# Reordering the attention's first rounds: cross values, the quantised layer and the input roundings of batches 1 to 3

## What is computed

```python
x = x + _L2_xattn_ref(_layernorm(x), ctx, ctx, ...)            # layer 5, E in the kernel
x = x + _L2_ffn_ref(_layernorm(x), weight, bias)               # layer 6, F
x = x + _L3_xattn_ref(_layernorm(x), ctx, ...)                 # layer 7, G

# layer 6: rows scaled by their largest value, rounded to whole numbers, times ternary weights
scale = jnp.maximum(jnp.max(jnp.abs(x), axis=-1, keepdims=True), eps) / 127.0
q_x = jnp.clip(jnp.round(x / scale), -128.0, 127.0) * scale
out = jnp.einsum('bsi,oi->bso', q_x, q_w) + bias

# layer 7: four inputs, each divided by its scale and rounded to fp8, 8 head groups
q = _ln(_fp8_linear_pertensor(ln_out, wq, wq_scale, q_in_scale).reshape(b, s, g, hpg, d), ...)
k = _ln(_fp8_linear_pertensor(ln_out, wk, ...)); v = _fp8_linear_pertensor(ln_out, wv, ...)
core = _gqa(q, k, v)
qx = _ln(_fp8_linear_pertensor(ln_out, wqx, ...))
kx, vx = jnp.split(jnp.einsum('bsi,oi->bso', cond, w_kv_x), 2, axis=-1)   # vx: the cross values
xout = _gqa(qx, _ln(kx), vx)
catq = _div_clamp_fp8(jnp.concatenate([core, xout], axis=-1), proj_smooth)
return jnp.einsum('bsi,oi->bso', catq, wproj) * (proj_in_scale * proj_w_scale)
```

## Time and profile before

| | |
|---|---|
| median of 3 runs | 1182.13 us (1180.92 to 1184.97) |
| profiled execution | 1181.37 us, its span 1179.3 us |
| TensorE matmuls busy | 1027.8 us, 87% |
| VectorE | 860.0 us, 73% |
| ScalarE | 626.6 us, 53% |
| GpSimd | 543.2 us, 46% |
| chain that ended last | TensorE 73%, VectorE 13%, ScalarE 7% |
| mean granted clock of TensorE | 0.934 of full speed |

### The profile page before, as it was taken

The page is one execution under the profiler, slowest core; times in us unless marked ns, Lnnn a source line. Parts: engine busy times, 40 slices in busy tenths (PEclk is TensorE's granted clock), DMA queues, the critical chain, the costliest instruction groups (busy, mean ns, idle before and its releaser), DMA issues.

```text
span 1179.3 us, 18867 instructions
## 1 busy us (share of the span) xinstructions
PE 1027.8 (87%) x6460; PEld 876.6 (74%) x6460; DVE 860.0 (73%) x2157; ACT 626.6 (53%) x1653; POOL 543.2 (46%) x408
## 2 busy tenths in 40 slices
PE   4999999999994978878479599999999999999936
PEld 4648888888883765555346488898889898999825
DVE  4437777777778536488986688988887888888653
ACT  1474444444332343678746457665767666666510
POOL 2316766677652222001245465556555656555520
PEclk9899999999997998888698799999999999999966
DMA  6002011011000101000000101010101000000011
GB/s 250 1 1 103 28 54 54 28 54 54 28 1 25 52 1 72 2 1 1 19 1 19 54 1 37 1 55 1 37 2 31 25 19 19 9 11 1 1 71 36
DMA packets 13630, 37.13 MB, mean 31 GB/s; under 512 B 1296, under 2 KB 5472, under 8 KB 12896
## 3 DMA queue, kind: packets, MB, share of 16 engines
q1 hardware_dynamic: 13536, 35.93, 9.2%
HBM read 34.88 MB, written 1.05 MB: 30 GB/s over the span
## 4 chain that ended last, share of the span: by engine, by line
PE 73%; DVE 13%; ACT 7%; issue 4%; POOL 1%; DMA 1%; SPq 0%; DVEq 0%; POOLq 0%; ACTq 0%
PE bank L677 15%; PE bank L2028 9%; PE bank L2016 9%; PE bank L1993 7%; PE bank L697 7%; PE bank L2040 4%; PE bank L1951 4%; PE bank L1038 2%; PE bank L1965 2%; PE bank L1053 1%; PE bank L487 1%; PE bank L488 1%; DMA cxT<-in_dram 1%; PE bank L1249 1%; DVE bst L240 1%
## 5 line engine op out<-in xcount | busy, mean ns | idle before, releaser
L2131 ACT ACTIVATE y<-bank,g_mx 128x256 f32<-128x256 f32 x256 | 117.2, 484 | 101.1 <-DVE g_mx L2272 87.9
L2368 POOL TENSOR_TENSOR y<-y,g_sm 128x1024 f32<-128x1024 f32 x64 | 119.8, 1893 | 21.8 <-DVE g_sm L2280 21.8
L2345 POOL TENSOR_TENSOR g_c<-arena 128x1024 fp32r<-128x1024 f32 x32 | 68.3, 2134 | 128.6 <-DVE arena L2250 128.6
L2016 PE MATMUL bank<-arena 128*128 128x256 f32 x512 | 116.0, 379 | 0.0
L715 ACT ACTIVATE arena<-arena 128x512 f32<-128x512 f32 x64 | 40.4, 632 | 125.6 <-DVE arena L796 125.5
L2016 PEld LDWEIGHTS bank<-arena 128*128 128x128 f32 x512 | 95.0, 190 | 11.9 <-issue 0.2
L677 PE MATMUL bank<-b_yh,b_wh 128*128 128x512 f32 x256 | 102.0, 398 | 0.0
L677 PE MATMUL bank<-b_yl,b_wh 128*128 128x512 f32 x256 | 101.4, 396 | 0.0
L677 PE MATMUL bank<-b_yh,b_wl 128*128 128x512 f32 x256 | 101.1, 395 | 0.0
L1993 PE MATMUL bank<-g_qh,g_xs 128*128 128x256 f32 x256 | 69.4, 306 | 22.3 <-POOL g_xs L2332 15.8
L750 POOL TENSOR_TENSOR b_hl<-arena,b_hh 128x512 fp32r<-128x512 f32 x64 | 81.3, 1291 | 10.3 <-ACT b_hh L724 10.3
(11 more groups left out here) (367 smaller groups left out, 3130.6 us busy)
## 6 DMA issues: line engine op xcount, KB each, us to landing
arena<-in_dram SPq DMA_DIRECT2D x37, 512.0 KB, 3.6
arena<-in_dram SPq DMA_DIRECT2D x17, 256.0 KB, 4.0
arena<-in_dram SPq DMA_DIRECT2D x3, 1024.0 KB, 7.8
cx<-in_dram SPq DMA_DIRECT2D x2, 1024.0 KB, 7.5
arena<-in_dram SPq DMA_DIRECT2D x2, 704.0 KB, 7.1
x<-in_dram SPq DMA_DIRECT2D x1, 1024.0 KB, 5.7
cxT<-in_dram SPq DMA_DIRECT2D x1, 1024.0 KB, 11.7
out_dram<-x SPq DMA_DIRECT2D x1, 1024.0 KB, 4.4
```

Of the source, the lines that this page charges most:

```text
L2016: m = pe.matmul(o[:, st * 256:st * 256 + 256], g_t[:, c, st * P:st * P + P], keys, start=True, stop=True)
L2131: m = act.activation(g_p[:, c, st, :], o[:, st * 256:st * 256 + 256], ACT.Exp, bias=g_mx[j % 2][:, 2 * c + st:2 * c + st + 1], accum_out=g ...
L2345: pool.tensor_tensor(cat, g_o[j % 2], g_om, ALU.subtract).then_inc(s_gc, 1)
L2368: pool.tensor_tensor(pf, pf, sums, ALU.mult).then_inc(s_gp, 1)
```

## The change

The same instructions are issued in another order, on TensorE, ScalarE, VectorE and GpSimd, for rounds 0 to 3; the bank table follows. V1 goes ahead of q(0), and its copies go ahead of E_rstd on ScalarE. Batch 3 of layer 6 goes into round 0 entirely: VectorE quantises it right after the statistics of round 0, TensorE does F_t and F_o behind V2. TensorE's yt2 goes ahead of q(1), yt3 behind sc(0); ScalarE scales batch 2 ahead of its work on kv(1) and takes batch 3's yt ahead of the exponentials. All roundings of batches 2 and 3 are in round 1 for VectorE and GpSimd (batch 3's were in round 3).

```diff
@@ -1509,6 +1509,7 @@
                     E_hT_act(act, s_ // 2 - 1)
             E_rows_act(act, 3)
             G_scale_act(act, 1)
+            cross_v_act(act, 1)
             E_rstd_act(act, 3)
 
         def E_centre_dve(dve, V):
@@ -1775,13 +1776,16 @@
 
         G_TRANSPOSES = (("pt", 0), ("tr", 0), ("pt", 1), ("tr", 2), ("tr", 1), ("pt", 2), ("pt", 3))
         CROSS = [tuple(("V", b, n // 2, n % 2) for n in range(4)) for b in range(B)]
-        G_EXTRA = {0: CROSS[1] + (("F", "t", 2), ("F", "o", 2)) + CROSS[2],
-                   1: (("G", "yt", 2), ("F", "t", 3), ("F", "o", 3)) + CROSS[3], 2: (("G", "yt", 3),)}
+        G_AHEAD = {0: CROSS[1], 1: (("G", "yt", 2),)}
+        G_EXTRA = {0: (("F", "t", 2), ("F", "o", 2)) + CROSS[2] + (("F", "t", 3), ("F", "o", 3)),
+                   1: (("G", "yt", 3),) + CROSS[3]}
         for i in range(NG + 3):
             for what, c in G_TRANSPOSES:
                 j = i - 2 if what == "pt" else i - 1
                 if 0 <= j < NG:
                     nxt(("G", what, j, c))
+            for key in G_AHEAD.get(i, ()):
+                nxt(key)
             if i < NG:
                 for c in range(2):
                     plan(("G", "q", i, c), c)
@@ -1976,6 +1980,11 @@
                         G_pt(pe, i - 2, c)
                     if what == "tr" and 0 <= i - 1 < NG:
                         G_tr(pe, i - 1, c)
+                if i == 0:
+                    pe.wait_ge(s_gwv1, 16)
+                    cross_v_pe(pe, 1, g_wvx[:, 0, :], g_wvx[:, 1, :])
+                if i == 1:
+                    yt_pe(pe, K_G, "G", (2,))
                 if i < NG:
                     g, b = i // B, i % B
                     if b == 0:
@@ -2042,18 +2051,14 @@
                                               stop=(c == 3 and w is g_pl))
                     fill(m, ("G", "pj", j))
                 if i == 0:
-                    pe.wait_ge(s_gwv1, 16)
-                    cross_v_pe(pe, 1, g_wvx[:, 0, :], g_wvx[:, 1, :])
                     F_t_pe(pe, 2)
                     F_o_pe(pe, 2)
                     cross_v_pe(pe, 2, g_wvx[:, 0, :], g_wvx[:, 1, :])
-                if i == 1:
-                    yt_pe(pe, K_G, "G", (2,))
                     F_t_pe(pe, 3)
                     F_o_pe(pe, 3)
+                if i == 1:
+                    yt_pe(pe, K_G, "G", (3,))
                     cross_v_pe(pe, 3, g_wvx[:, 0, :], g_wvx[:, 1, :])
-                if i == 2:
-                    yt_pe(pe, K_G, "G", (3,))
 
         G_PT_DVE = (0, 2)
 
@@ -2106,6 +2111,9 @@
                         G_pt_act(act, i - 2, c)
                     if what == "tr" and 0 <= i - 1 < NG:
                         G_tr_act(act, i - 1, c)
+                if i == 1:
+                    G_yt_act(act, 2)
+                    G_scale_act(act, 2)
                 if i < NG:
                     if i >= 3:
                         take(act, ("G", "pv", i - 3, 1))
@@ -2118,8 +2126,11 @@
                                                  o[:, 256:512].rearrange("p (g d) -> p g d", g=2), ACT.Identity,
                                                  scale=row("s_v")), ("G", "kv", i, tt))
                 if i == 0:
-                    cross_v_act(act, 1)
+                    F_qT_act(act, 2)
+                    cross_v_act(act, 2)
                     split_p_act(act, 0)
+                if i == 1:
+                    G_yt_act(act, 3)
                 if 0 <= i - 1 < NG:
                     j = i - 1
                     if j >= 1:
@@ -2156,16 +2167,10 @@
                         empty(m, ("G", "pv", j, a))
 
                 if i == 0:
-                    F_qT_act(act, 2)
-                    cross_v_act(act, 2)
+                    F_qT_act(act, 3)
                 if i == 1:
-                    G_yt_act(act, 2)
-                    F_qT_act(act, 3)
-                    G_scale_act(act, 2)
+                    G_scale_act(act, 3)
                     cross_v_act(act, 3)
-                if i == 2:
-                    G_yt_act(act, 3)
-                    G_scale_act(act, 3)
                 if i == 3:
                     act.wait_ge(s_gx, 16)
                     split_w_act(act, 1, BOTH)
@@ -2232,8 +2237,6 @@
                         take(dve, ("G", "pv", i - 3, 1))
                     if 0 in G_PT_DVE:
                         G_pt_dve(dve, i - 2, 0)
-                if i == 3:
-                    G_round_dve(dve, V, 3, (0,))
                 if 0 <= i - 3 < NG:
                     j = i - 3
                     have(dve, ("G", "pv", j, 0))
@@ -2251,8 +2254,6 @@
                 if 0 <= i - 2 < NG:
                     if 2 in G_PT_DVE:
                         G_pt_dve(dve, i - 2, 2)
-                if i == 3:
-                    G_round_dve(dve, V, 3, (1,))
                 if i < NG:
                     for tt in range(2):
                         o = take(dve, ("G", "q", i, tt))
@@ -2271,6 +2272,11 @@
                         o = take(dve, ("G", "sc", j, c))
                         dve.tensor_reduce(g_mx[j % 2][:, 2 * c:2 * c + 2], o[:, :].rearrange("p (q s) -> p q s", q=2),
                                           AX.X, ALU.max, negate=True).then_inc(s_gnb, 1)
+                if i == 0:
+                    ln_scale(dve, K_F, 3)
+                    F_quant_dve(dve, V, 3)
+                if i == 1:
+                    G_round_dve(dve, V, 2, (0,))
                 for tt in range(2):
                     if 0 <= i - 1 < NG:
                         j = i - 1
@@ -2292,17 +2298,15 @@
                     F_add_dve(dve, V, 2)
                     ln_open_batch(dve, V, 2)
                     G_round_dve(dve, V, 1, (1,))
-                    ln_scale(dve, K_F, 3)
-                    F_quant_dve(dve, V, 3)
                     ln_scale(dve, K_G, 2)
                     F_bias_dve(dve, V, 3)
-                    split_p_dve(dve, 0)
-                if i == 1:
                     F_add_dve(dve, V, 3)
                     ln_open_batch(dve, V, 3)
-                    G_round_dve(dve, V, 2, (0,))
+                    split_p_dve(dve, 0)
                     ln_scale(dve, K_G, 3)
+                if i == 1:
                     G_round_dve(dve, V, 2, (1,))
+                    G_round_dve(dve, V, 3)
                 if i == 2:
                     centre_w_dve(dve, V, 1)
                 if i == 3:
@@ -2333,9 +2337,6 @@
 
         def G_pool(pool, C):
             for i in range(NG + 3):
-                if i == 3:
-                    G_round_pool(pool, 3, (0,))
-                    pool.wait_ge(s_gx, 14)
                 if i >= 3:
                     j = i - 3
                     pool.wait_ge(s_gt, j + 1)
@@ -2343,8 +2344,6 @@
                     if j >= 2:
                         take(pool, ("G", "pj", j - 2))
                     pool.tensor_tensor(cat, g_o[j % 2], g_om, ALU.subtract).then_inc(s_gc, 1)
-                if i == 3:
-                    G_round_pool(pool, 3, (1,))
                 if i < NG:
 
                     pool.wait_ge(s_gst, i + 1)
@@ -2359,6 +2358,9 @@
                     G_round_pool(pool, 1, (0,))
                     ln_pool(pool, C, K_G, EPS, twice=True, batches=(2,))
                     G_round_pool(pool, 1, (1,))
+                    ln_pool(pool, C, K_G, EPS, twice=True, batches=(3,))
+                if i == 1:
+                    G_round_pool(pool, 2, (0,))
                 if 1 <= i <= NG:
                     j = i - 1
                     for half in range(2):
@@ -2367,8 +2369,8 @@
                         sums = g_sm[j % 2][:, 4 * half:4 * half + 4].unsqueeze(2).to_broadcast([P, 4, 256])
                         pool.tensor_tensor(pf, pf, sums, ALU.mult).then_inc(s_gp, 1)
                 if i == 1:
-                    ln_pool(pool, C, K_G, EPS, twice=True, batches=(3,))
-                    G_round_pool(pool, 2)
+                    G_round_pool(pool, 2, (1,))
+                    G_round_pool(pool, 3)
                 if i == 2:
                     centre_w_pool(pool, 1)
                 if B <= i < NG - B and i % B == 0:
```

## The result

| | median | lowest to highest | profiled execution, its span | granted clock |
|---|---|---|---|---|
| before | 1181.95 us | 1180.92 to 1184.97, 4 runs | 1181.4, 1179.3 | 0.934 |
| after | 1172.27 us | 1171.07 to 1173.74, 4 runs | 1171.9, 1169.9 | 0.937 |

The ratio is 0.9916 (95% 0.9899 to 0.9934), a gain of 9.7 us, by the interval 7.8 to 11.9. The forecast was 1171.7.

A forecast was written before the change was run, and what follows sets the result against it. TensorE bound the kernel from 663.11 us; before that, q(3) waited for batch 3's rounded inputs. sc(2) 10.95 us earlier (8.8 wait, 2.15 clock), less VectorE's lateness, gave 10.4: 1182.1 - 10.4 = 1171.7 us, range 1165 to 1180.

The forecast's parts named there:

- The lock: On VectorE, a rounding with two of its three tensor_scalars held beside GpSimd's subtracts takes 4.0 us instead of 2.55.
- Step 1, V1: V1's eight pairs start at 575.04, behind the recurrent layer's last transposes, and end 583.5; cost nothing, E_rstd 0.1 us late.
- Rival B: V1 ahead runs at 1.2 GHz throughout, E_rstd 5.1 us late: gain 5.3, 1176.8 us; chance 0.13.
- Step 2, round 0: Batch 3's quantising goes into VectorE's 2.36 us wait; yt2 at 607.65, q(1) starts at 608.65, 1.35 us later.
- Step 3, round 1: First exponential at 619.4 instead of 615.06; three VectorE roundings in a row, n=5 to 7, end at 637.3.
- Step 4, the cut: In round 2 TensorE idles about 8.3 us for VectorE's pt(0,0) copy behind the roundings; pt(0,3) at 638.0, q(3) at 654.3.
- The sum: sc(2) 10.95 us earlier (8.8 wait, 2.15 clock); sc(2) to q(4) 12.9 us instead of 12.3; gain 10.4 us.
- Rival C: Freed rounds meet VectorE's order and 7 us or more return by round 5; about 1180 us, chance 0.07.
- Rival A: Held tensor_scalars don't add up: roundings of 2.55 end at 631.5, pt(0,3) follows at once; 1163 us, chance 0.10.
- D: Holes of rounds 0 to 2 keep TensorE at 1.2 GHz from 608.65 until q(3): 8.4 us slower, 1190.5; chance 0.08.

The follow-up runs named there:

- no_lock: after with GpSimd's subtracts of roundings n=5 and n=6 left out and plain ScalarE copies in their place; 1170.93 us, ratio 0.9903.
- late_split: after with VectorE's split of the next batch's values moved to the following round, behind its copies and ahead of q's statistics; 1176.14 us.
- v1_only: before with V1 alone put ahead of q(0), its copies ahead of E_rstd; 1182.09 us, ratio 1.0003.
- warm: after with one value tile each of batches 2 and 3 moved between round 1's transposes and yt2, F_o(3) in another bank; 1173.93 us.
- copies_first: after with batch 3's two VectorE roundings moved behind round 2's two copies of transposed probabilities; 1166.81 us, ratio 0.9872.

## Why the prediction was right

**The lock.** Confirmed by no_lock. n=6 and n=7 took 4.17 and 4.18 us (4.0 forecast), n=5 5.77 (5.45). The Trainium skill, GPSIMD Engine Reference, its opening table, says that VectorE contends in a 2-port mode or with two SBUF inputs. With the second half this case's rows agree, as the next figures show. For the first they show one-input tensor_scalars that are held, but no row names the mode. I had given the bias add, which has two such inputs, up to 1.2 us, a figure that no row gives. It took 1.64 beside GpSimd's subtract, against 0.68 alone, off the path, and late_split's subtract, also with two, took 2.77 against 1.21.

**Step 1, V1.** It ran 572.89 to about 581.3, with 1.71 and 1.57 us for the first two pairs and 0.86 a pair from 576.17 on: 583.3 in the prediction's time (583.5). That end owes something to luck. The row that the rise was taken from was read early: in before the clock was still 0.50 from 625.10 to 626.20, so it rose some 4.7 us after 621.72 and not four, and here it rose some 3.2 us after V1 began. E_rstd was not late: VectorE took its result at 585.49, 587.44 in the prediction's time (587.42 before). Rival B is refuted, by v1_only as well. The Trainium skill, ScalarE: Activation LUTs, What ACT_TABLE_LOAD costs, would have added a drain to each load:

```profile
582.12 1.28 ACT L1463 ACT_TABLE_LOAD   x1
583.42 0.32 ACT L1463 ACTIVATE e_r<-e_r,e_eps 128x32 f32<-128x32 f32 x1
583.76 1.28 ACT L1465 ACT_TABLE_LOAD   x1
585.05 0.23 ACT L1465 ACTIVATE e_r<-e_r 128x32 f32<-128x32 f32 x1
```

The Exp starts 0.01 us after its load ended, so no drain shows and the measurement decides.

**Step 2, round 0.** F_quant(3) went into the hole (591.73 to 595.17), as said. One reason was missed: F_o3 waited 4.03 us for VectorE's add of batch 2 (L1706), which empties the bank that F_o3 takes in the round robin. I had only asked when its data (f_qT) came. So the clock fell earlier than forecast: it was 0.56 with F_o3 and 0.50 with round 1's transposes (until 603.0), 1.00 again with yt2, and 0.50 over most of q(1). It cost nothing more, as warm shows. yt2 came at 605.41 (607.36 in the prediction's time, 607.65 forecast).

**Step 3, round 1.** The first exponential came at 616.77 (618.7; 619.4), right behind the yt copy of 615.86. The roundings ended at 635.43 (637.4; 637.3).

**Step 4, the cut.** pt(0,3) came at 636.17 (638.1; 638.0) after 9.18 us of idle (8.3), released by VectorE's pt copy, and copies_first, which takes that wait away, gains what it should. q(3) followed without a wait at 2.4 GHz (3.83 us). sc(2) was 10.81 us earlier (10.95).

**The sum.** From sc(2) to q(4) after takes 13.17 us (12.9 forecast), and at q(4) the lead is 9.97 us (from the entry 95.15 against 105.12), 10.35 forecast. The steps stand there. Behind q(4) I assumed no change, and that does not hold: the lead is 8.4 us at sc(4) and 7.45 at the end. Before had an idle of 2.39 us in round 5 too, at 696.53, and its clock stayed up:

```profile
696.53 1.16 PE L1951 MATMUL bank<-cst,y 128*128 128x128 f32 x8 [2.39 <-DVE x L2228]
```

After's idle of 2.41 us at 684.63 is followed by transposes of 1.55 and a q of 3.06 us. The granted clock of these stretches, before first:

```profile
696.50:699.60 3.10, 3.07 (x25) 2.98 (x26) 2.93 (x5) 0.59 (x1) 1.44 (x3) 1.00 0.02 5
```

```profile
684.60:689.10 4.50, 4.47 (x25) 4.38 (x26) 4.33 (x9) 0.59 (x1) 2.42 (x4) 0.62 0.00 0
```

It returns at 807.50 and 930.37 in after; before has one such q, at 940.78 (3.37 us). At 807.50 the idles are equal as well, after first:

```profile
807.50 1.54 PE L1955 MATMUL bank<-cst,y 128*128 128x128 f32 x8 [1.82 <-DVE x L2233]
```

```profile
818.04 1.16 PE L1951 MATMUL bank<-cst,y 128*128 128x128 f32 x8 [1.82 <-DVE x L2228]
```

Counted from the entry, the lead is 9.95 us at the transposes of round 5 and 8.59 two rounds later, still 8.59 at 807.50 and 7.24 two rounds behind it. From there to the end it stays between 7.15 and 7.45, since the third fall is in both kernels. So the one term that failed is that for all behind q(4), zero in the sum: in this execution it was a loss of 2.7 us to two more falls of the clock, some 1.35 us each, and 0.3 us came back at the very end. In the second execution, with one fall more than before, 8.0 us are left at the end.

That the median still fell 0.6 us from the forecast is in part luck. The medians give 9.7 us and, for the second run of after, 7.8 (0.9934 of 1181.95), and those of one kernel differ by 1.85 us (1172.27 and 1174.12). Of the 9.4 us between the spans of the two profiled executions, 1.95 lie ahead of the entry, and are not the change's. Rival C had the direction, not the size or the reason. Rival A is refuted by the tensor_scalars over 1 us, D by pv(0) at full clock (3.45 us).

**Open.** Why the clock falls in one timing and not in the other, behind idles of the same length, isn't settled. In the ten profiled executions of changed orders that keep the idle of 2.39 to 2.41 us in round 5 it fell there each time, in before and v1_only not. In late_split, where that idle is 1.25 us, it stayed up; whether the length did it, or the timing, isn't shown. Nor is it known why the entry differs by up to 2.7 us between kernels whose VectorE work up to there is the same.

## What to carry to other kernels

When work is moved forward into an engine's gap, ask which copies in its new queue empty a bank or buffer, and put these first: batch 3's roundings were worth 7.7 us at sc(2) in round 1 and 13 behind two copies of 0.65 us. A wait for data and a wait for the bank are two questions, and both must be asked of every moved step. Price an elementwise instruction by who runs beside it, and of a move check what it costs at its new place: the same subtract cost 1.21 us at one and 2.77 at another.

## What was not expected of the hardware

- Contention between VectorE and GpSimd goes both ways. GpSimd's small 128x2 tensor_scalar L304 at 608.90 took 1.07 us beside VectorE's subtract L1945, which has two inputs in SBUF; a like one at 601.40 took 0.24. VectorE then waited 0.87 us for the result.
- A full-size VectorE subtract with two SBUF inputs more than doubled (1.21 to 2.77 us) beside a GpSimd subtract of 2.13 us, while 128x1024 bf16 tensor_scalars end about 0.3 us after GpSimd's instruction, whatever is left of it (0.43 to 1.26, 1.33 or 2.00 us).
- Idles of TensorE of the same length with the same work around them left the clock up in one kernel and down in the other: 2.39 us in round 5 (before at 696.53, the second execution of after at 685.34), and 1.82 us at 818.04 in before and 807.50 in after.
